# Retrieval stage: gate products as 64x32 tiles in four groups of 16 token pairs, scores in two halves

## The chip, the cores and the metric

The kernel runs on one core of one Trainium2 chip. The number that counts is device time in microseconds, the median of three runs; the profile is one further execution of the same program. Everything is float32, and a float32 product of the program stands in the trace as two LDWEIGHTS and two MATMUL (two passes).

## The reference, cut to what matters

The program is a whole two-layer perceiver block on 64 sequences of 32 tokens with 256 features (2048 tokens). The change touches one of its six parts, the feed-forward by retrieved experts of layer 0:

```python
sim = einsum('pbnhd,hkpd->pbnhk', q, keys)          # 2 x 8 heads x 64 keys per token
sx, ix = top_k(sim[0], 8);  sy, iy = top_k(sim[1], 8)
scores, pk = top_k(all pairs sx + sy, 8)            # 8 picks for each of 8 heads
indices = 64 * ix + iy, picked by pk                # one of 4096 experts
h = gelu(einsum('bnd,bnhkd->bnhk', x, down_embed[indices]))
out = einsum('bnhk,bnhkd->bnd', softmax(scores) * h, up_embed[indices])
```

A token has 64 picks, each an expert number and a weight.

## The kernel before, in words

Function `retrieve` does not gather experts. For each tile of 128 tokens it computes gelu(x · down) for all 4096 experts (`gh`, 128 expert rows x 32 expert columns x 128 tokens), multiplies it by a gate (the summed softmax weights, zero where an expert is not picked), and multiplies by the whole `up` table. The gate of a token is a product of two one-hot matrices over its picks: `row_hot` (pick x 128 rows) and `col_hot` (pick x column, times the weight).

Before the change two neighbouring tokens share one product: the 128 partitions hold the 64 picks of an even and the 64 of an odd token, `col_hot` has 64 columns (32 expert columns x parity of the token), and one matmul (L1262) contracts all 128 partitions into 128 x 64 gate values. 64 pairs make eight groups of eight; a group fills one PSUM bank, and two banks (5 and 6) take turns.

The stage is a software pipeline over 16 tiles, driven by `skewed`: in one step tile x is normalised, turned and scored, tile c (one behind) gets its hidden products and its picks, tile t (two behind) its gates, tile o (three behind) its output product. Steps 0 to 5 and the last three are written out; steps 6 to 15 are a hardware loop of five passes whose body is two steps. There is no planner: the order on each engine is as written, with semaphores between engines.

The step of TensorE (PE) has eight slices. In slice i, in this order: 4 `up` products of tile o (L1287, N=256), 8 `down` products of tile c (L1298, N=128), in slice 0 the turning of x (L1277), in slice 2 both score halves (L1270, banks 1 and 2), and gate group i (L1262), which waits for `weighted` of group i-2, for its `row_hot` and its `col_hot`. At the end of the step the picks are turned (L1310, bank 7).

VectorE (DVE), in slice i: `weigh(i-1)` (L1450: `gh` times a gate bank), `hot(i)` (L1436 compare; in even slices L1439, the near `row_hot`; L1442 times the weight), then a piece of the top-k of tile c (`share`). `scored` (L1454) is in slice 4. ScalarE (ACT), in slice i: in even slices 8 Abs (L1328, `rows_apart`) for the next odd group, the gelu of slice i (L1340), then Relu (L1334, the far `row_hot`). An Exp in slice 5 needs a table load each way.

Of the kernel before, what the change touches and what calls it, by code (L numbers as in the profile page):

```python
# [15 lines left out]
P = 128  # L16
# [7 lines left out]
C = 512  # L24
# [1165 lines left out]
def retrieve(nc, g, banks, n, pairs, offset, tables):  # L1190
# [7 lines left out]
    GROUPS, GP = 8, 8  # L1198
    CH = NE // GROUPS
    down, up = tables["down"], tables["up"]  # L1200
    with ExitStack() as ctx:
        s = Scope(nc, ctx, "s3e")
        sb = s.sb
        count, parity = sb("count", [P, K]), sb("parity", [P, 1])
# [13 lines left out]
        upper, low = sb("upper", [P, M]), sb("low", [P, M])  # L1218
# [4 lines left out]
        apart = sb("apart", [P, GP, P])  # L1223
        col_hot = sb("col_hot", [P, 2, GP, M])
# [5 lines left out]
        Y_BANK, S_BANK, H_BANK, G_BANK, T_BANK = 0, 1, 3, 5, 7  # L1230
# [3 lines left out]
        def half(t, i):  # L1234
            return t.b * (GROUPS // 2) + i // 2 + 1
# [16 lines left out]
        @block.tensor  # L1252
        def _(pe):
            def step(item):
                x, c, t, o = item(LAG_X), item(LAG_C), item(LAG_E), item(LAG_Y)

                def gate(i):
                    after(pe, weighted, group(t, i - 2))
                    pe.wait_ge(far_rows if i % 2 else near_rows, half(t, i))
                    pe.wait_ge(cols_ready, group(t, i))  # L1260
                    for j in range(GP):
                        mm = pe.matmul(banks[:, G_BANK + i % 2, j * M:(j + 1) * M], lhsT=row_hot[:, i % 2, j, :], rhs=col_hot[:, i % 2, j, :], start=True, stop=True)  # L1262
                    mm.then_inc(gate_ready, 1)

                def score():
                    pe.wait_ge(xT_ready, x.b + 1)
                    after(pe, sim_ready, x.b)
                    for j in range(2):
                        for k in range(KT):
                            mm = pe.matmul(banks[:, S_BANK + j, :], lhsT=xT[:, x.u, k, :], rhs=pairs[:, k, j * C:(j + 1) * C], start=k == 0, stop=k == KT - 1)  # L1270
                    mm.then_inc(sims, 1)

                def x_transposed():
                    pe.wait_ge(xn_ready, x.b + 1)
                    after(pe, picksT_ready, x.b - 1)
                    for k in range(KT):
                        mm = pe.transpose(banks[:, T_BANK, tok(k)], xn[:, x.u, tok(k)], g.ident[:])  # L1277
                    mm.then_inc(x_tr, 1)
                for i in range(GROUPS):
                    if o:  # L1280
                        if i == 0 and first(o):
                            pe.wait_ge(tables["up_loaded"], 16)
                        if i == 0:
                            pe.wait_ge(weighted, group(o, GROUPS - 1))
                            after(pe, added, o.b)
                        for e in range(i * CH, (i + 1) * CH):
                            mm = pe.matmul(banks[:, Y_BANK, 0:D], lhsT=gh[:, o.u, e, :], rhs=up[:, e, :], start=e == 0, stop=e == NE - 1)  # L1287
                        if i == GROUPS - 1:
                            mm.then_inc(summed, 1)
                    if c:  # L1290
                        if i == 0 and first(c):
                            pe.wait_ge(tables["down_loaded"], 16)
                        if i == 0:
                            pe.wait_ge(xT_ready, c.b + 1)
                        after(pe, gelu_ready, group(c, i - 2))
                        for e in range(CH):
                            for k in range(KT):
                                mm = pe.matmul(banks[:, H_BANK + i % 2, tok(e)], lhsT=down[:, k, i * CH + e, :], rhs=xT[:, c.u, k, :], start=k == 0, stop=k == KT - 1)  # L1298
                        mm.then_inc(hidden, 1)
# [6 lines left out]
                    if c and i == GROUPS - 1:  # L1306
                        pe.wait_ge(picks_ready, c.b + 1)
                        pe.wait_ge(xT_ready, c.b + 2 if x else NT)
                        for j in range(3):
                            mm = pe.transpose(banks[:, T_BANK, tok(j)], picks[:, j, :, :].rearrange("p r m -> p (r m)"), g.ident[:])  # L1310
                        mm.then_inc(picks_tr, 1)
            skewed(pe, NT, 3, step)

        @block.scalar
        def _(act):
            act.wait_ge(const_loaded, 48)
            act.wait_ge(set_up, 1)

            def step(item):
                x, c, t = item(LAG_X), item(LAG_C), item(LAG_E)  # L1320

                def rows_apart(i):
                    if i == 1:
                        act.wait_ge(picksT_ready, t.b + 1)
                    after(act, far_rows, half(t, i) - 1)
                    for j in range(GP):
                        q = i * GP + j
                        ins = act.activation(apart[:, j, :], number[:], ACT.Abs, bias=picksT[:, t.u, 0, q:q + 1], scale=-1.0)  # L1328
                    ins.then_inc(apart_ready, 1)

                def rows_hot(i):
                    act.wait_ge(apart_ready, half(t, i))
                    after(act, gate_ready, group(t, i - 2))
                    act.activation(row_hot[:, 1, :, :], apart[:], ACT.Relu, bias=one[:], scale=-1.0).then_inc(far_rows, 1)  # L1334
# [23 lines left out]
        def _(dve):  # L1358
            link = Link(dve, dve_link)
            dve.wait_ge(const_loaded, 48)  # L1360

            def step(item):
                x, c, t, o = item(LAG_X), item(LAG_C), item(LAG_E), item(LAG_Y)

                def best_of(first):
                    if first == 0:
                        dve.wait_ge(sim_ready, c.b + 1)
# [51 lines left out]
                def keys():  # L1419
# [6 lines left out]
                    link(dve.scalar_tensor_tensor(low[:], upper[:], -float(NE), key[:, 1, :], ALU.mult, ALU.add))  # L1426
                    dve.tensor_scalar(picks[:, 1, :, :], bc(low[:].unsqueeze(1), P, 2, M), 2.0, parity[:], ALU.mult, ALU.add).then_inc(picks_ready, 1)
# [3 lines left out]
                def hot(i):  # L1431
                    qs = slice(i * GP, (i + 1) * GP)
# [3 lines left out]
                    dve.tensor_tensor(col_hot[:, i % 2, :, :], bc(number[:, 0:M].unsqueeze(1), P, GP, M), bc(picksT[:, t.u, 1, qs].unsqueeze(2), P, GP, M),  # L1436
                                      ALU.is_equal).then_inc(cols_hit, 1)
                    if i % 2 == 0:
                        dve.tensor_tensor(row_hot[:, 0, :, :], bc(number[:].unsqueeze(1), P, GP, P), bc(picksT[:, t.u, 0, qs].unsqueeze(2), P, GP, P),  # L1439
                                          ALU.is_equal).then_inc(near_rows, 1)  # L1440
                    dve.wait_ge(cols_hit, group(t, i))
                    dve.tensor_tensor(col_hot[:, i % 2, :, :], col_hot[:, i % 2, :, :], bc(picksT[:, t.u, 2, qs].unsqueeze(2), P, GP, M),  # L1442
                                      ALU.mult).then_inc(cols_ready, 1)

                def weigh(i):
                    mine = gh[:, t.u, :, i * 2 * GP:(i + 1) * 2 * GP].rearrange("p e (q r) -> p e q r", r=2)
                    if i == 0:
                        dve.wait_ge(gelu_ready, group(t, GROUPS - 1))
                    dve.wait_ge(gate_ready, group(t, i))
                    dve.tensor_tensor(mine, banks[:, G_BANK + i % 2, :].rearrange("p (q e r) -> p e q r", q=GP, r=2), mine, ALU.mult).then_inc(weighted, 1)  # L1450
                def scored():
                    dve.wait_ge(sims, x.b + 1)
                    after(dve, sim_read, x.b - 1)
                    dve.tensor_tensor(sim[:, x.u, :, :].rearrange("p c k -> p (c k)"), banks[:, S_BANK:S_BANK + 2, :].rearrange("p n c -> p (n c)"), offset[:], ALU.add).then_inc(sim_ready, 1)  # L1454
# [5 lines left out]
                for i in range(GROUPS):  # L1460
# [9 lines left out]
                if o:  # L1470
                    dve.wait_ge(summed, o.b + 1)
# [6 lines left out]
            skewed(dve, NT, 3, step, link, 17)  # L1478
# [1297 lines left out]
```

## Time and profile before

| | us |
|---|---|
| three runs | 3247.96, 3250.59, 3251.38 |
| median | 3250.59 |
| the profiled execution, its own time | 3256.49 |
| its span, first to last instruction | 3254.7 |
| mean granted TensorE clock | 0.935 |
| busy: PE 2775.6, weight load (PEld) 2163.4, DVE 2127.2, ACT 1503.7, GpSimd 649.0 | |

The span is 1.8 us shorter than the profiled execution's time, and that execution is 5.9 us above the median. The retrieval lies from about 933 to 1737 us of the span. In the profile PE rows are matmuls, whose ends are modelled, and PEld rows are weight loads. In a merged row of several loads, the first starts at the row's start and the last ends at start plus duration.

### The profile page before, as it was taken

The numbers are of one execution on the slowest core, as the hardware profiler recorded it, in microseconds if no ns is written. First come the engines' busy times: TensorE is split into PE (matmuls) and PEld (weight loads), VectorE is DVE, ScalarE is ACT, GpSimd is POOL, SyncE is SP. The second block draws the span as 40 slices with busy tenths as digits, with TensorE's granted clock in tenths as the row PEclk, the third lists the DMA queues.
The fourth block names the chain that finished last, engine by engine and source line by source line (L and its number), as shares of the span: only waits on it lengthen the run. The fifth ranks groups of instructions, "written<-read, shape, count | busy, mean of one in ns | idle before, by whom it ended". The sixth has DMA issues, their size and how long they took to land. (4 is left out here: it accounts for less than half of the span.)

```text
span 3254.7 us, 64318 instructions
## 1 busy us (share of the span) xinstructions
PE 2775.6 (85%) x21884; PEld 2163.4 (66%) x21885; DVE 2127.2 (65%) x5161; ACT 1503.7 (46%) x4075; POOL 649.0 (20%) x809
## 2 busy tenths in 40 slices
PE   6699996999779999999997999995737777769993
PEld 3588884666668888889884777773323333569993
DVE  6588885666347777777772777775459999832222
ACT  3555552555224444444450777771366766113331
POOL 3355552122000000000000222220032222012224
PEclk8899998999879999999998999997859999969997
DMA  3122221000300000000000111111200000261112
GB/s 91 50 68 63 66 65 41 1 0 0 162 1 1 1 1 0 0 0 0 0 1 21 33 29 32 32 27 38 97 0 1 1 1 1 104 256 36 35 37 89
DMA packets 69088, 120.54 MB, mean 37 GB/s; under 512 B 10192, under 2 KB 51504, under 8 KB 64368
## 3 DMA queue, kind: packets, MB, share of 16 engines
q1 hardware_dynamic: 65568, 109.76, 10.2%
q0 software_dynamic: 3408, 9.31, 1.0%
q8 instruction: 67, 1.10, 0.1%
q14 instruction: 45, 0.37, 0.0%
HBM read 99.19 MB, written 17.69 MB: 36 GB/s over the span
## 5 line engine op out<-in xcount | busy, mean ns | idle before, releaser
L1262 PEld LDWEIGHTS s_ps<-s3e_col_hot,s3e_row_hot 128*128 128x128 f32 x2048 | 240.9, 192 | 36.6 <-issue 27.8
L1262 PE MATMUL s_ps<-s3e_col_hot,s3e_row_hot 128*128 128x64 f32 x2048 | 247.2, 274 | 21.1 <-DVE s3e_col_hot L1442 20.3
L1287 PE MATMUL s_ps<-s_up,s3e_gh 128*128 128x256 f32 x1024 | 252.8, 392 | 7.3 <-DVE s3e_gh L1450 7.3
L1298 PEld LDWEIGHTS s_ps<-s3e_xT,s_down 128*128 128x128 f32 x2048 | 249.9, 193 | 7.1 <-issue 1.1
L1298 PE MATMUL s_ps<-s3e_xT,s_down 128*128 128x128 f32 x2048 | 251.1, 277 | 0.0
L1340 ACT ACTIVATE s3e_gh<-s_ps 128x512 f32<-128x512 f32 x128 | 76.3, 597 | 364.1 <-PE s_ps L1298 363.9
L1287 PEld LDWEIGHTS s_ps<-s_up,s3e_gh 128*128 128x128 f32 x1024 | 188.1, 193 | 32.4 <-DVE s3e_gh L1450 10.5
L1450 DVE TENSOR_TENSOR s3e_gh<-s_ps,s3e_gh 128x512 f32<-128x512 f32 x128 | 88.3, 690 | 180.2 <-PE s_ps L1262 180.2
L1691 ACT ACTIVATE s4b_pr<-s4b_sc,s4b_nm 128x257 f32<-128x257 f32 x256 | 127.8, 503 | 114.9 <-DVE s4b_nm L1739 114.8
L2594 ACT ACTIVATE s6e_hT<-s_ps,s_b 128x128 f32<-128x128 f32 x312 | 84.9, 383 | 186.9 <-PE s_ps L2567 186.9
L2235 DVE SCALAR_TENSOR_TENSOR s5c_fresh<-s_ps,s5c_state 128x1024 f32<-128x1024 f32 x124 | 151.4, 1221 | 13.9 <-PE s_ps L2189 7.5
L191 POOL MEMSET s4q_half<- 128x1 f32 x1 | 0.1, 99 | 804.1 <-POOLq L2689 804.1
L1328 ACT ACTIVATE s3e_apart<-s3e_number,s3e_picksT 128x128 f32<-128x128 f32 x512 | 156.0, 388 | 1.6
L2567 PEld LDWEIGHTS s_ps<-s6e_xT,s6e_w 128*128 128x128 f32 x1248 | 146.7, 193 | 5.5 <-ACT s6e_xT L2598 3.5
L2567 PE MATMUL s_ps<-s6e_xT,s6e_w 128*128 128x128 f32 x1248 | 147.2, 277 | 2.9 <-ACT s6e_xT L2598 2.9
L2618 DVE TENSOR_TENSOR s6e_y<-s_ps,s_b 128x256 f32<-128x256 f32 x39 | 16.6, 425 | 198.5 <-PE s_ps L2581 198.5
L670 PE MATMUL p_ps<-s_wc,s1b_cT 96*128 96x256 f32 x512 | 128.1, 394 | 20.0 <-DMA s1b_cT<-ctxT 20.0
L2581 PE MATMUL s_ps<-s_w,s6e_hT 128*128 x624 | 141.2, 379 | 0.8 <-DVE s6e_y L2618 0.8
L2241 DVE TENSOR_TENSOR s5c_fresh<-s5c_fresh,s_ps 128x2048 f32<-128x2048 f32 x62 | 141.2, 2278 | 0.0
L2040 ACT ACTIVATE s5c_decay<-s5b_dt,s_rate 128x128 f32<-128x128 f32 x384 | 113.8, 389 | 45.9 <-PE s_ps L2189 44.2
L1643 PE MATMUL s_ps<-s4a_wv,s4b_cT 96*128 96x256 f32 x512 | 123.1, 384 | 4.4 <-DMA s4b_cT<-ctxT 4.4
L2581 PEld LDWEIGHTS s_ps<-s_w,s6e_hT 128*128 128x128 f32 x624 | 115.5, 190 | 15.3 <-issue 1.2
(428 smaller groups left out, 6630.9 us busy)
## 6 DMA issues: line engine op xcount, KB each, us to landing
s_w<-p_w SPq DMA_DIRECT2D x16, 1024.0 KB, 13.5
s4b_cT<-ctxT SPq DMA_DIRECT2D x64, 192.8 KB, 2.4
s1b_cx<-ctx SPq DMA_DIRECT2D x64, 192.0 KB, 2.7
s1b_cT<-ctxT SPq DMA_DIRECT2D x64, 192.0 KB, 2.9
s_results<-s6e_y SPq DMA_DIRECT2D x39, 128.0 KB
s_down<-p_down SPq DMA_DIRECT2D x1, 4096.0 KB, 22.0
s_up<-p_up SPq DMA_DIRECT2D x1, 4096.0 KB, 31.2
s_silu_z<-s5p_sz SPq DMA_DIRECT2D x4, 1024.0 KB, 4.5
```

Of the source, the lines that this page charges most:

```text
L670: mm = pe.matmul(banks[:, K_BANK + c.u, j * D:(j + 1) * D], lhsT=cT[:, c.u, k, tok(j)], rhs=wc[:, k, 0:D], start=k == 0, stop=k == 1)
L1262: mm = pe.matmul(banks[:, G_BANK + i % 2, j * M:(j + 1) * M], lhsT=row_hot[:, i % 2, j, :], rhs=col_hot[:, i % 2, j, :], start=True, stop= ...
L1287: mm = pe.matmul(banks[:, Y_BANK, 0:D], lhsT=gh[:, o.u, e, :], rhs=up[:, e, :], start=e == 0, stop=e == NE - 1)
L1298: mm = pe.matmul(banks[:, H_BANK + i % 2, tok(e)], lhsT=down[:, k, i * CH + e, :], rhs=xT[:, c.u, k, :], start=k == 0, stop=k == KT - 1)
L1328: ins = act.activation(apart[:, j, :], number[:], ACT.Abs, bias=picksT[:, t.u, 0, q:q + 1], scale=-1.0)
L1643: mm = pe.matmul(banks[:, V_BANK, j * D:(j + 1) * D], lhsT=cT[:, d.u, k, tok(j)], rhs=wv[:, k, :], start=k == 0, stop=k == 1)
L1691: ins = act.activation(pr[:, e.u, n, :], sc[:, e.u, n, :], ACT.Exp, bias=nm[:, e.u, n:n + 1], accum_out=sums[:, bass.ds(e.b, 1), n])
L2040: return act.activation(decay[:, t % 2:t % 2 + steps, k, :, n, :], steps_of(dt, k, t, steps), ACT.Exp, scale=rate[:, k, n:n + 1])
L2235: dve.scalar_tensor_tensor(part_of(fresh, h, part, 2), banks[:, D_BANK:D_BANK + 2, :].rearrange("p j d -> p (j d)"), floor, part_of(state, ...
L2241: dve.tensor_tensor(part_of(fresh, h, 0, HG), part_of(fresh, h, 0, HG), banks[:, I_BANK:I_BANK + HG, :].rearrange("p j d -> p (j d)"), ALU ...
L2567: mm = pe.matmul(banks[:, H_BANK + 2 * m.u + f // 4, tok(f % 4)], lhsT=w[:, m.u, k, tok(f)], rhs=xT[:, m.u, k, :], start=k == 0, stop=k == ...
L2581: mm = pe.matmul(banks[:, Y_BANK, 0:D], lhsT=hT[:, o.u, f, :], rhs=w2[:, bass.ds(e, 1), f, :], start=f == 0, stop=f == FT - 1)
```

## The change

- Gates: each token has a product of its own. Four column tiles of 32 expert rows times two row tiles of 64 partitions make 8 products of 64x32 weights with N=32 per pair, in place of one of 128x128 with N=64. The even token writes one bank, the odd token another. `col_hot` has 32 columns; the parity input and `low` are gone.
- Groups: four of 16 pairs instead of eight of 8, one every second slice, each in two banks (4/5 and 6/7). In every group the first 8 pairs have a near `row_hot` (DVE) and the last 8 a far one (ACT), so that the far one is needed by every group.
- PE's order: `down` before `up` in each slice; the gate's waits (`gate_inputs`) stand ahead of `up` in odd slices, the gate itself at the slice's end.
- ACT's gelu of slice i now waits for `up` of slice i too, since both tiles share the `gh` buffer.
- Scores: halves in slices 2 and 5 through bank 1, which also serves both turnings; `scored` in slices 3 and 7. The picks' turning waits for the second half to be read.

```diff
-    GROUPS, GP = 8, 8
-    CH = NE // GROUPS
+    SLICES, GROUPS, GP, HP = 8, 4, 16, 8
+    CH = NE // SLICES
+    GC = 32
...
-        col_hot = sb("col_hot", [P, 2, GP, M])
+        col_hot = sb("col_hot", [P, 2, GP, NE])
...
-        Y_BANK, S_BANK, H_BANK, G_BANK, T_BANK = 0, 1, 3, 5, 7
+        Y_BANK, T_BANK, H_BANK, G_BANK = 0, 1, 2, 4
...
-            for dst, src in ((count, "count8"), (parity, "parity"), (number, "row_no")):
+            for dst, src in ((count, "count8"), (number, "row_no")):
...
+                def gate_inputs(i):
+                    after(pe, weighted, group(t, i - 2))
+                    pe.wait_ge(near_rows, group(t, i))
+                    pe.wait_ge(far_rows, group(t, i))
+                    pe.wait_ge(cols_ready, group(t, i))
+
                 def gate(i):
-                    after(pe, weighted, group(t, i - 2))
-                    pe.wait_ge(far_rows if i % 2 else near_rows, half(t, i))
-                    pe.wait_ge(cols_ready, group(t, i))
                     for j in range(GP):
-                        mm = pe.matmul(banks[:, G_BANK + i % 2, j * M:(j + 1) * M], lhsT=row_hot[:, i % 2, j, :], rhs=col_hot[:, i % 2, j, :], start=True, stop=True)
+                        for g in range(P // GC):
+                            for r in range(2):
+                                ms, cs = slice(r * M, (r + 1) * M), slice(g * GC, (g + 1) * GC)
+                                mm = pe.matmul(banks[cs, G_BANK + 2 * (i % 2) + r, j * NE:(j + 1) * NE], lhsT=row_hot[ms, i % 2, j, cs], rhs=col_hot[ms, i % 2, j, :],
+                                               start=True, stop=True)
                     mm.then_inc(gate_ready, 1)
...
+                    if t and i % 2:
+                        gate_inputs(i // 2)
...
                     if x and i == 2:
-                        score()
-                    if t:
-                        gate(i)
+                        score(0)
+                    if x and i == 5:
+                        score(1)
+                    if t and i % 2:
+                        gate(i // 2)
                     if c and i == GROUPS - 1:
...
-                        pe.wait_ge(xT_ready, c.b + 2 if x else NT)
+                        pe.wait_ge(sim_ready, 2 * c.b + 4 if x else 2 * NT)
...
-                for i in range(GROUPS):
+                for i in range(SLICES):
                     if t and i % 2 == 0:
-                        rows_apart(i + 1)
+                        rows_apart(i // 2)
                     if c:
-                        act.wait_ge(hidden, group(c, i))
+                        act.wait_ge(hidden, part_of(c, i))
+                        if o:
+                            act.wait_ge(summed, part_of(o, i))
...
                     if t and i % 2 == 0:
-                        rows_hot(i + 1)
+                        rows_hot(i // 2)
...
-                for i in range(GROUPS):
-                    if t:
+                for i in range(SLICES):
+                    if t and i % 2 == 0:
                         if i:
-                            weigh(i - 1)
-                        hot(i)
-                    if x and i == 4:
-                        scored()
+                            weigh(i // 2 - 1)
+                        hot(i // 2)
+                    if x and i == 3:
+                        scored(0)
+                    if x and i == 7:
+                        scored(1)
```

## Rows read from the trace of the kernel before

**Rows 1.** The page, costliest groups: the loads of the gate and of `down`.

```profile
L1262 PEld LDWEIGHTS s_ps<-s3e_col_hot,s3e_row_hot 128*128 128x128 f32 x2048 | 240.9, 192 | 36.6 <-issue 27.8
L1298 PEld LDWEIGHTS s_ps<-s3e_xT,s_down 128*128 128x128 f32 x2048 | 249.9, 193 | 7.1 <-issue 1.1
```

**Rows 2.** Windows: one step of the loop, from one turning of picks to the next.

```profile
core 0: us, PE busy (x) PEld busy (x) DVE busy (x) ACT busy (x) POOL busy (x), PEclk, DMA share, GB/s
1299.79:1347.84 48.05, 47.10 (x336) 42.90 (x334) 36.53 (x124) 22.11 (x50) 0.00 (x0) 1.00 0.00 0
```

**Rows 3.** Timeline, weight loads of one slice: start, duration, name, idle before.

```profile
1325.69 1.60 PEld L1287 LDWEIGHTS s_ps<-s_up,s3e_gh 128*128 128x128 f32 x8
1327.32 1.97 PEld L1298 LDWEIGHTS s_ps<-s3e_xT,s_down 128*128 128x128 f32 x16
1329.20 1.87 PEld L1262 LDWEIGHTS s_ps<-s3e_col_hot,s3e_row_hot 128*128 128x128 f32 x16
1330.99 1.60 PEld L1287 LDWEIGHTS s_ps<-s_up,s3e_gh 128*128 128x128 f32 x8
```

**Rows 4.** Timeline where two steps meet.

```profile
1299.77 0.69 DVE L1450 TENSOR_TENSOR s3e_gh<-s_ps,s3e_gh 128x512 f32<-128x512 f32 x1 [1.76 <-PE s_ps L1262]
1300.51 1.59 PEld L1287 LDWEIGHTS s_ps<-s_up,s3e_gh 128*128 128x128 f32 x8 [0.69 <-DVE s3e_gh L1450]
```

**Rows 5.** Timeline, loads of a burst of 128x32 weights, N=32, in phase 1.

```profile
302.49 0.22 PEld L662 LDWEIGHTS p_ps<-s1b_pT,s1b_vv 128*32 128x32 f32 x16 [0.39 <-ACT s1b_pT L723]
...
302.84 0.17 PEld L662 LDWEIGHTS p_ps<-s1b_pT,s1b_v 128*32 128x32 f32 x7
303.05 0.30 PEld L670 LDWEIGHTS p_ps<-s_wc,s1b_cT 96*128 96x128 f32 x2
```

**Rows 6.** Groups by form: busy us, mean ns of one load in the two bursts.

```profile
L662 PEld LDWEIGHTS p_ps<-s1b_pT,s1b_vv 128*32 128x32 f32 x2048 | 29.1, 112 | 25.6 <-ACT s1b_pT L723 13.6 <-issue 12.0
L1676 PEld LDWEIGHTS s_ps<-s4b_kT,s4b_qb 32*64 32x64 f32 x1024 | 15.4, 129 | 44.8 <-DVE s4b_nm L1739 26.8 <-issue 13.7 <-ACT s4b_kT L1703 4.3
```

**Rows 7.** Timeline, loads of a burst with row tiles (32x64 weights) in phase 4.

```profile
2002.22 0.24 PEld L1676 LDWEIGHTS s_ps<-s4b_kT,s4b_qb 32*64 32x64 f32 x16 [0.95 <-DVE s4b_nm L1739]
```

**Rows 8.** Groups by form, 1300 to 1670 us: DVE's and ACT's parts around the gate.

```profile
L1450 DVE TENSOR_TENSOR s3e_gh<-s_ps,s3e_gh 128x512 f32<-128x512 f32 x62 | 42.8, 690 | 84.9 <-PE s_ps L1262 84.9
L1442 DVE TENSOR_TENSOR s3e_col_hot<-s3e_col_hot,s3e_picksT 128x512 f32<-128x512 f32 x62 | 42.7, 689 | 1.1
L1436 DVE TENSOR_TENSOR s3e_col_hot<-s3e_number,s3e_picksT 128x512 f32<-128x512 f32 x62 | 42.2, 681 | 0.0
L1439 DVE TENSOR_TENSOR s3e_row_hot<-s3e_number,s3e_picksT 128x1024 f32<-128x1024 f32 x31 | 37.8, 1219 | 0.0
```

**Rows 9.** Timeline, ACT and DVE beside the slice of Rows 3.

```profile
1324.71 2.43 ACT L1328 ACTIVATE s3e_apart<-s3e_number,s3e_picksT 128x128 f32<-128x128 f32 x8
...
1328.29 0.68 DVE L1442 TENSOR_TENSOR s3e_col_hot<-s3e_col_hot,s3e_picksT 128x512 f32<-128x512 f32 x1
...
1329.51 0.60 ACT L1340 ACTIVATE s3e_gh<-s_ps 128x512 f32<-128x512 f32 x1 [2.37 <-PE s_ps L1298]
1330.01 1.14 ACT L1334 ACTIVATE s3e_row_hot<-s3e_apart,s3e_one 128x1024 f32<-128x1024 f32 x1
```

**Rows 10.** DMA queue of instructions, first 1040 to 1250 us, then 1252 to 1650 us.

```profile
q8 instruction: 12, 0.20, 0.4%
...
q8 instruction: 1, 0.02, 0.0%
```

**Rows 11.** DMA issues, the shortest time to landing: size, then us.

```profile
s6r_rw<-p_rw SPq DMA_DIRECT2D x1, 8.0 KB, 1.6
```

**Rows 12.** Timeline at the start of the retrieval.

```profile
933.44 0.42 SPq L1246 DMA_DIRECT2D s3e_parity<-parity  x1
...
935.78 0.41 DVE L169 TENSOR_SCALAR s3e_xn<-x_rows,s_mv,s_rstd 128x256 f32<-128x256 f32 x1 [20.61 <-DMA s3e_number<-row_no]
```

More of the change, by code:

```diff
@@ L1203, in retrieve @@
         sb = s.sb
-        count, parity = sb("count", [P, K]), sb("parity", [P, 1])
+        count = sb("count", [P, K])
         number = sb("number", [P, P])
@@ L1217, in retrieve @@
         ex, den, rden = sb("ex", [P, H, K]), sb("den", [P, H]), sb("rden", [P, H])
-        upper, low = sb("upper", [P, M]), sb("low", [P, M])
+        upper = sb("upper", [P, M])
         picks = sb("picks", [P, 3, 2, M])
@@ L1222, in retrieve @@
         row_hot = sb("row_hot", [P, 2, GP, P])
-        apart = sb("apart", [P, GP, P])
-        col_hot = sb("col_hot", [P, 2, GP, M])
+        apart = sb("apart", [P, HP, P])
+        col_hot = sb("col_hot", [P, 2, GP, NE])
         gh = sb("gh", [P, U, NE, P])
@@ L1229, in retrieve, with part_of @@
             "apart_ready near_rows far_rows cols_hit cols_ready gate_ready weighted hidden gelu_ready summed added")
[L1230 removed]
+        Y_BANK, T_BANK, H_BANK, G_BANK = 0, 1, 2, 4
         LAG_X, LAG_C, LAG_E, LAG_Y = range(4)
         block = ctx.enter_context(nc.Block())
[L1234 to L1235 removed]
+        def part_of(t, i):
+            return t.b * SLICES + i + 1
         def group(t, i):
@@ L1255, in step, with score @@
                 x, c, t, o = item(LAG_X), item(LAG_C), item(LAG_E), item(LAG_Y)
+                def gate_inputs(i):
[3 more added lines that the diff above has]
+                    pe.wait_ge(cols_ready, group(t, i))
                 def gate(i):
-                    after(pe, weighted, group(t, i - 2))
-                    pe.wait_ge(far_rows if i % 2 else near_rows, half(t, i))
-                    pe.wait_ge(cols_ready, group(t, i))
                     for j in range(GP):
-                        mm = pe.matmul(banks[:, G_BANK + i % 2, j * M:(j + 1) * M], lhsT=row_hot[:, i % 2, j, :], rhs=col_hot[:, i % 2, j, :], start=True, stop=True)
-                    mm.then_inc(gate_ready, 1)
[L1265 to L1270, printed above, removed]
+                        for g in range(P // GC):
[3 more added lines that the diff above has]
+                                               start=True, stop=True)
+                    mm.then_inc(gate_ready, 1)
+                def score(j):
+                    if j:
+                        pe.wait_ge(sim_ready, 2 * x.b + 1)
+                    else:
+                        pe.wait_ge(xT_ready, x.b + 1)
+                    for k in range(KT):
+                        mm = pe.matmul(banks[:, T_BANK, :], lhsT=xT[:, x.u, k, :], rhs=pairs[:, k, j * C:(j + 1) * C], start=k == 0, stop=k == KT - 1)
                     mm.then_inc(sims, 1)
@@ L1275, in x_transposed @@
                     after(pe, picksT_ready, x.b - 1)
+                    after(pe, sim_ready, 2 * x.b)
                     for k in range(KT):
@@ L1278, in x_transposed @@
                     mm.then_inc(x_tr, 1)
-                for i in range(GROUPS):
+                for i in range(SLICES):
+                    if c:
+                        if i == 0 and first(c):
+                            pe.wait_ge(tables["down_loaded"], 16)
+                        if i == 0:
+                            pe.wait_ge(xT_ready, c.b + 1)
+                        after(pe, gelu_ready, part_of(c, i - 2))
+                        for e in range(CH):
+                            for k in range(KT):
+                                mm = pe.matmul(banks[:, H_BANK + i % 2, tok(e)], lhsT=down[:, k, i * CH + e, :], rhs=xT[:, c.u, k, :], start=k == 0, stop=k == KT - 1)
+                        mm.then_inc(hidden, 1)
+                    if t and i % 2:
+                        gate_inputs(i // 2)
                     if o:
@@ L1287, in step @@
                             mm = pe.matmul(banks[:, Y_BANK, 0:D], lhsT=gh[:, o.u, e, :], rhs=up[:, e, :], start=e == 0, stop=e == NE - 1)
[L1288 to L1299, printed above, removed]
+                        mm.then_inc(summed, 1)
                     if x and i == 0:
@@ L1315, in _ @@
         def _(act):
-            act.wait_ge(const_loaded, 48)
+            act.wait_ge(const_loaded, 32)
             act.wait_ge(set_up, 1)
             def step(item):
-                x, c, t = item(LAG_X), item(LAG_C), item(LAG_E)
+                x, c, t, o = item(LAG_X), item(LAG_C), item(LAG_E), item(LAG_Y)
                 def rows_apart(i):
-                    if i == 1:
+                    if i == 0:
                         act.wait_ge(picksT_ready, t.b + 1)
-                    after(act, far_rows, half(t, i) - 1)
-                    for j in range(GP):
-                        q = i * GP + j
+                    after(act, far_rows, group(t, i) - 1)
+                    for j in range(HP):
+                        q = i * GP + HP + j
                         ins = act.activation(apart[:, j, :], number[:], ACT.Abs, bias=picksT[:, t.u, 0, q:q + 1], scale=-1.0)
@@ L1331, in rows_hot @@
                 def rows_hot(i):
-                    act.wait_ge(apart_ready, half(t, i))
+                    act.wait_ge(apart_ready, group(t, i))
                     after(act, gate_ready, group(t, i - 2))
-                    act.activation(row_hot[:, 1, :, :], apart[:], ACT.Relu, bias=one[:], scale=-1.0).then_inc(far_rows, 1)
-                for i in range(GROUPS):
+                    act.activation(row_hot[:, i % 2, HP:GP, :], apart[:], ACT.Relu, bias=one[:], scale=-1.0).then_inc(far_rows, 1)
+                for i in range(SLICES):
                     if t and i % 2 == 0:
-                        rows_apart(i + 1)
+                        rows_apart(i // 2)
                     if c:
-                        act.wait_ge(hidden, group(c, i))
+                        act.wait_ge(hidden, part_of(c, i))
+                        if o:
+                            act.wait_ge(summed, part_of(o, i))
                         act.activation(gh[:, c.u, i * CH:(i + 1) * CH, :].rearrange("p e q -> p (e q)"), banks[:, H_BANK + i % 2, :], ACT.Gelu_apprx_tanh).then_inc(gelu_ready, 1)
                     if t and i % 2 == 0:
-                        rows_hot(i + 1)
+                        rows_hot(i // 2)
                     if x and i == 0:
@@ L1425, in keys @@
                     dve.scalar_tensor_tensor(picks[:, 0, :, :], bc(key[:, 0, :].unsqueeze(1), P, 2, M), 2.0, bc(upper[:].unsqueeze(1), P, 2, M), ALU.mult, ALU.add)
-                    link(dve.scalar_tensor_tensor(low[:], upper[:], -float(NE), key[:, 1, :], ALU.mult, ALU.add))
-                    dve.tensor_scalar(picks[:, 1, :, :], bc(low[:].unsqueeze(1), P, 2, M), 2.0, parity[:], ALU.mult, ALU.add).then_inc(picks_ready, 1)
+                    dve.scalar_tensor_tensor(picks[:, 1, :, :], bc(upper[:].unsqueeze(1), P, 2, M), -float(NE), bc(key[:, 1, :].unsqueeze(1), P, 2, M),
+                                             ALU.mult, ALU.add).then_inc(picks_ready, 1)
                 pieces = (lambda: best_of(H), candidates, lambda: places_of(0), lambda: places_of(H), top_of, positions, hits, soften, keys)
@@ L1431, in hot @@
                 def hot(i):
-                    qs = slice(i * GP, (i + 1) * GP)
+                    qs, near = slice(i * GP, (i + 1) * GP), slice(i * GP, i * GP + HP)
                     if i == 0:
@@ L1447, in weigh, with scored @@
                     if i == 0:
-                        dve.wait_ge(gelu_ready, group(t, GROUPS - 1))
+                        dve.wait_ge(gelu_ready, part_of(t, SLICES - 1))
                     dve.wait_ge(gate_ready, group(t, i))
[L1450 to L1454, printed above, removed]
+                    both = banks[:, G_BANK + 2 * (i % 2):G_BANK + 2 * (i % 2) + 2, :]
+                    dve.tensor_tensor(mine, both.rearrange("p r (q e) -> p e q r", q=GP), mine, ALU.mult).then_inc(weighted, 1)
+                def scored(j):
+                    dve.wait_ge(sims, 2 * x.b + j + 1)
+                    if j == 0:
+                        after(dve, sim_read, x.b - 1)
+                    dve.tensor_tensor(sim[:, x.u, j * H:(j + 1) * H, :].rearrange("p c k -> p (c k)"), banks[:, T_BANK, :], offset[:, j * C:(j + 1) * C], ALU.add).then_inc(sim_ready, 1)
                 if x:
@@ L1459, in step @@
                     best_of(0)
-                for i in range(GROUPS):
-                    if t:
+                for i in range(SLICES):
+                    if t and i % 2 == 0:
                         if i:
-                            weigh(i - 1)
-                        hot(i)
-                    if x and i == 4:
-                        scored()
+                            weigh(i // 2 - 1)
[4 more added lines that the diff above has]
+                        scored(1)
                     if c:
@@ L1477, in step @@
                     dve.bn_stats(g.stats[:, o.b, :], X[:, o.b, :])
-            skewed(dve, NT, 3, step, link, 17)
+            skewed(dve, NT, 3, step, link, 16)
 def phase4(nc, g):
```

17 lines of the change are left out of this document (8 added, 9 removed).

## The prediction

> **What bounds the kernel now.** I read the page's groups first, then one step by windows, then the timeline of one slice. In the groups the gate's weight loads take as long as those of `down`, 241 and 250 us, though its products have N=64 against 128 [rows 1]: a 128x128 load costs 118 ns (240.9 / 2048), and N=64 hides under it. The windows say whose time it is: a step lasts 48.05 us, PE is busy for 47.10 at full clock, DVE for 36.5, ACT for 22.1 [rows 2]. So whatever leaves PE shortens the step until DVE, at 36.5, or a chain through DVE and ACT is late. In the slice, loads start at 1325.69 (`up`), 1327.32 (`down`), 1329.20 (gate) and 1330.99 (`up`): 1.63 + 1.88 + 1.79 = 5.30 us [rows 3]. Two gate groups are 3.58 us; four such pairs make 14.3 us of a step. The only real gap is where steps meet: `up` waits 0.69 us for the last `weigh` [rows 4].
>
> **The new gate on PE.** A group of 16 pairs is 16 x 8 products = 128, two passes each = 256 loads and 256 matmuls, in place of 32 and 32. The trace has no 64x32 burst. The nearest is 128x32 with N=32 [rows 5]: 48 passes, first load at 302.49, the last seven begin at 302.84 and end 0.17 later; a load of this form lasts 0.112 [rows 6], so the last starts at 302.90: 0.41 us for 47 steps, 8.7 ns each. Its first 16 need (0.22 - 0.11)/15 = 7.3 ns, and so do 16 loads over row tiles (0.24 - 0.13, /15) [rows 6, 7], so row tiles bring no penalty. From first load to the next line's load are 0.56 us for 48, 11.7 ns each with the change of shape at the end. Bounds for a group: 256 x 7.3 = 1.9 us and 256 x 11.7 = 3.0 us. I take 256 x 8.7 = 2.2, plus 0.15 at the exit (0.56 - 0.41) and 0.1 at the entry, whose load can't slip under the matmul before: 2.5 us. Against 3.58 a group saves 1.08 us, a step 4.3 us.
>
> The burst in the trace is short, and its 8.7 ns a pass need tiles that work side by side [rows 5]. The Trainium skill, TensorEngine Tiling (Array Packing), section Instruction Overhead, says that each matmul has about 60 cycles of overhead and that one shouldn't take a tiling factor from a dimension that is already small. This change does just that; by that rule, an estimate, a pass would be 25 ns and a group 6.4 us. The row shows passes of a third of that, so it speaks against; it stays as a rival.
>
> **Instruction supply.** This is the term that I can't read directly. PE's instructions per step are 336 + 334 = 670 now [rows 2]; the change takes 4 x 64 away and adds 4 x 512: 2462. Between 1040 and 1250 us, written-out steps and the loop's first pass, the instruction queue moved 12 packets of 16 KB, one per 17.5 us, or 17.5 x 670/48 = 244 instructions: a packet is about 256 instructions of 64 bytes. From 1252 to 1650 us, the other four passes of the loop, it moved one [rows 10]. So the body of 1340 instructions is kept. A body of 4924 may not be; then each pass fetches again, 10 packets a step. A group's 512 instructions are two packets used up in 2.2 us, 1.1 us each. A packet takes 0.4% x 16 x 210 / 12 = 1.12 us of a DMA engine [rows 10], just even. If the next is asked for only when the one before it is entered, the time to landing counts: the shortest in the trace is 1.6 us, for 8 KB [rows 11]. If 0.3 of that is data (a guess) and 1.12 stands in its place, it is 2.4. Then one packet per group comes late by 2.4 - 1.1 = 1.3 us. Bounds: 0 and 1.3 us per group. I take 0.45, nearer to the packet's own row, since some instructions are queued ahead. A step: +1.8 us. Each jump back of the loop, four of them, may wait for its target: bounds 0 and 2.4, I take 1.5: +6 us in all.
>
> The Trainium skill, Runtime: NRT & Kernel Launch, section Instruction fetch mechanics, gives PE room for 2048 instructions, refilled in blocks of 256, the next fetched while the current runs, and a wait at a taken branch outside that window. The trace agrees on the block (244) and doesn't show the room. By it the loop is refetched and the wait is not zero.
>
> **The waits put ahead of `up`.** In a double slice, PE's loads now run `down` 0 to 1.88, `up` to 3.51, `down` to 5.39, then the gate's waits with `up` and the gate queued behind them. The far `row_hot` is ready when? ACT's gelu of the even slice waits for `up`'s matmuls, whose end is 0.06 + 1.95 after its first load at 1.88: 3.9. Gelu to Relu takes 0.50 and the Relu 1.14 [rows 9]: 5.55, the wait seen at 5.6 and the first load at 5.65 to 5.7. That is 0.3 late. In slice 0 the turning of x, in slice 2 the score half give cover, so 2 of 4 double slices pay: +0.6 us a step; bounds 0 and 4 x 0.3. The 8 Abs (2.43) start after the odd gelu of the double slice before, and are done long before 3.9.
>
> On DVE: gate end, `weigh` over 1024 columns 1.22 (as L1439, the same width), compare 0.6, near rows 1.15, product 0.69 [rows 8], ready about 4.0 after the double slice starts, needed at 5.4. In slice 0 the statistics, the normalisation and eight MAX8 come first, but also the turned picks and x on PE; ready about 0.6 us ahead of need. Bounds: 0, and 0.5 us a step if it isn't; I take 0.
>
> **Where steps meet.** `down` (1.88 us) now stands before `up`, and `weigh` grows from 0.69 to 1.22: it ends about 1.35 us after the gate, the picks' turning and `down` cover 2.3. The gap of 0.69 goes [rows 4]: -0.6 us a step. The picks' turning waits for `scored(1)` in slice 7, behind `keys` on DVE; DVE has 1 us to spare there, bounds 0 and 1 us.
>
> **The rest.** DVE loses 4 x (0.68 + 0.69) for `col_hot`, 8 x 0.69 becomes 4 x 1.22 for `weigh`, `low` goes (0.2), two half `scored` cost 0.2 more: 36.5 to about 30.4 us, below the new step. It is worth nothing by itself; it only keeps DVE from bounding. The score passes are the same eight; their bank is read between the halves, two slices apart. Parity's DMA goes from the start, 0.42 us of issue ahead of the load that DVE waits for [rows 12]: -0.4 us once.
>
> **Sum.** A step with a tile in t: -4.3 + 1.8 + 0.6 - 0.6 = -2.5 us, 16 such steps: -40. Loop jumps +6, parity -0.4: -34 us. Against the profiled execution's own 3256.5 that gives 3222.5; it stands 5.9 above the median of 3250.6, which I forecast: 3217.
>
> **Rivals.**
> 1. Supply is no limit. Loads as above, no late packet, no wait at jumps: -4.3 us a step, 16 x = -69: 3182; at 7.3 ns a pass 3160. For it: PE ran 96 instructions in 0.41 us without a hitch [rows 5]. Against: those fit a queue, 512 don't. Chance 0.17.
> 2. The other side: instruction supply bounds the gate. One late packet per group. From 0.95 us on (64 x 0.95 = 61 of delay, plus 6 to 10 for jumps, against 69 saved) the change is not faster; at 1.3 it gives 64 x 1.3 + 4 x 2.4 - 69 = +24: 3274. For it: the landing time [rows 11] and a body 3.7 times as long. Against: a packet's 1.12 us. Chance 0.27.
> 3. The inputs bound: far rows, `col_hot` or the picks come about 1 us late in each double slice, because a wait ahead of `up` stops everything behind it. 64 x 0.7 of delay beyond the sum: 3262. For it: already now `col_hot` ends at 1328.97 and its gate starts at 1329.20 [rows 3, 9]. Against: the sums above. Chance 0.1.
> 4. The tiles' loads run one after another: 32 columns cost a quarter of the 118 ns of 128 [rows 1], 29 ns a pass, 7.5 us a group: 64 x (7.5 - 2.5) = +320 from the sum: 3537. Against: 8.7 ns in the burst [rows 5]. Chance 0.04. (The page on tiling would have it so, near enough.)
>
> My forecast has 0.42: late packets of 0.2 to 0.8 us per group, 3195 to 3243. A measurement can tell about 0.2%, 6.5 us, from no change. Faster (below 3244): 0.42 + 0.17, less 0.05 for the upper edge = 0.54. Within: 0.05 from there and 0.05 from rivals 2 and 3: 0.1. Slower: 0.36. The range is 3172 to 3285: it leaves out rival 4 and the tails of 1 and 2.
>
> **What would show it.** A loop step of 45.5 us by the turning of picks (43.7 in rival 1, about 49.5 in rival 2). L1262's successor with 16384 loads, 256 of a group within 2.2 us; a hole of over 0.5 us amid a group, near an instruction packet, speaks for supply, and instruction packets every 4 to 5 us all through the loop say that the body isn't kept. No hole and 8.7 ns: rival 1. The wait of `up` on ACT's far rows in slices 5 and 7, about 0.3 us each. No wait of `up` on `weigh` where steps meet. DVE near 30 us a step. The forecast is wrong if passes run at over 12 ns in an unbroken burst, or if holes exceed 0.9 us.

## The result: 3383.8 us, 4.1% slower

The changed kernel takes 3383.81 us (median of four runs, 3378.16 to 3386.72) against 3249.47 for the kernel before on the same chip: ratio 1.0411, 95% interval 1.0393 to 1.0429. The forecast was 3217, faster, with a range up to 3285. It was wrong in its sign and in its range. The profiled execution took 3378.16 us with a span of 3376.4, which is 121.7 above the span before.

First the page of the changed kernel: weight loads of the gate (L1269), `down` (L1298) and `up` (L1309). Behind the bars stand busy us and mean ns, then idle time ahead and what ended it.

```profile
L1269 PEld LDWEIGHTS s_ps<-s3e_col_hot,s3e_row_hot 64*32 64x32 f32 x16384 | 151.9, 106 | 162.5 <-issue 162.2
L1298 PEld LDWEIGHTS s_ps<-s3e_xT,s_down 128*128 128x128 f32 x2048 | 286.5, 221 | 36.1 <-issue 32.4
L1309 PEld LDWEIGHTS s_ps<-s_up,s3e_gh 128*128 128x128 f32 x1024 | 198.5, 204 | 40.8 <-issue 11.1
```

The `up` loads of the kernel before, which the groups ahead don't show:

```profile
L1287 PEld LDWEIGHTS s_ps<-s_up,s3e_gh 128*128 128x128 f32 x1024 | 188.1, 193 | 32.4 <-DVE s3e_gh L1450 10.5 <-issue 0.6
```

With [rows 1] these rows say where the time went. Gate: busy -89.0, idle +125.9. `down`: busy +36.6, idle +29.0. `up`: +10.4 and +8.4. The sum is +121.3 us. That it equals the growth of the span, 121.7, is in part chance: the retrieval, from its first weight load to the end of its last, grew from 798.8 to 929.9 us, by 131.1, and the rest of the program, which the change doesn't touch, was 9.4 shorter in this execution. The other 10 us of the retrieval lie in its smaller products and where rows overlap. So the gate's loads became cheaper, as forecast, and the gate's idle time, nearly all "issue" (waiting for nothing that the profile shows), grew by 126 us.

Two steps of it by windows, the columns as in [rows 2]. The first (step 7) ends the loop's first pass, the second (step 8) begins with the first jump back.

```profile
1233.44:1286.98 53.54, 46.08 (x1231) 40.29 (x1229) 30.86 (x111) 22.12 (x50) 0.00 (x0) 0.94 0.01 3
1286.98:1346.79 59.81, 46.75 (x1238) 40.35 (x1230) 30.85 (x111) 22.12 (x50) 0.00 (x0) 0.91 0.01 3
```

PE is now busy for 46 of 53 to 60 us, where it was busy for 47.10 of 48.05; DVE fell from 36.5 to 30.9, as forecast (30.4). The timeline of the loads shows the holes. Columns: start, duration, instructions, idle before.

```profile
1280.71 1.59 PEld L1309 LDWEIGHTS s_ps<-s_up,s3e_gh 128*128 128x128 f32 x8
1282.64 1.50 PEld L1269 LDWEIGHTS s_ps<-s3e_col_hot,s3e_row_hot 64*32 64x32 f32 x166 [0.33 <-issue]
1286.08 0.86 PEld L1269 LDWEIGHTS s_ps<-s3e_col_hot,s3e_row_hot 64*32 64x32 f32 x90 [1.95 <-issue]
1286.98 0.31 PEld L1323 LDWEIGHTS s_ps<-x_ident,s3e_picks 128*128 128x128 f32 x3
1291.68 3.48 PEld L1298 LDWEIGHTS s_ps<-s3e_xT,s_down 128*128 128x128 f32 x16 [4.39 <-issue]
1295.04 3.00 PEld L1309 LDWEIGHTS s_ps<-s_up,s3e_gh 128*128 128x128 f32 x8
1298.07 0.36 PEld L1287 LDWEIGHTS s_ps<-x_ident,s3e_xn 128*128 128x128 f32 x2
1298.39 1.86 PEld L1298 LDWEIGHTS s_ps<-s3e_xT,s_down 128*128 128x128 f32 x16
```

The burst of 256 loads runs at 8 to 9 ns each, stops for 1.95 us, and goes on. Over all 64 bursts the mean length, from the start of the first load to that of the last, is 4.36 us; the shortest, unbroken, take 2.14, and 60 of the 64 have at least one hole. So the holes cost 64 x 2.22 = 142 us in all. The second thing is at 1286.98: the loop jumps back, and the next `down` starts 4.4 us later and takes 3.48 us instead of 1.86. Windows of the stretches with the clock (third column from the end): the wait at the jump, `down` and `up` behind it, the next slice.

```profile
1286.98:1291.60 4.62, 0.55 (x11) 0.31 (x3) 4.50 (x14) 3.09 (x10) 0.00 (x0) 0.57 0.04 7
1291.60:1298.10 6.50, 6.42 (x24) 5.86 (x25) 4.01 (x28) 0.00 (x0) 0.00 (x0) 0.52 0.01 3
1298.39:1301.80 3.41, 3.41 (x26) 3.23 (x25) 0.00 (x0) 1.91 (x3) 0.00 (x0) 1.00 0.00 0
```

A granted clock of 0.52 is the lower of the two levels, 1.2 GHz, for nearly the whole stretch: it fell while PE idled at the jump, stayed low while `down` and `up` ran, and is 1.00 in the slice behind them. In the kernel before a step of the loop had it at 1.00 [rows 2]. Over the whole retrieval the trace has the lower level for 177 us, where the kernel before had it for 24. Last, the instruction queue from 1300 to 1700 us, all in the loop:

```profile
q8 instruction: 72, 1.18, 1.3%
```

72 packets, one per 5.6 us, where the kernel before had one in the last four passes of its loop, 400 us [rows 10]: the loop's body is no longer kept.

### The profile page after: what moved, and what is told of

Same layout as the page of the kernel before. It is cut to its first block and busy times, and to the rows that moved or that the text cites. A ratio compares the mean times of both kernels' runs of the same rounds, so it can differ in the third digit from the quotient of the medians.

```text
span 3376.4 us, 92832 instructions
## 1 busy us (share of the span) xinstructions
PE 2774.1 (82%) x36220; PEld 2133.2 (63%) x36221; DVE 2035.5 (60%) x4969; ACT 1503.9 (45%) x4075; POOL 645.4 (19%) x809
## 5 line engine op out<-in xcount | busy, mean ns | idle before, releaser
L1298 PE MATMUL s_ps<-s3e_xT,s_down 128*128 128x128 f32 x2048 | 300.2, 308 | 21.2 <-issue 21.2
L1298 PEld LDWEIGHTS s_ps<-s3e_xT,s_down 128*128 128x128 f32 x2048 | 286.5, 221 | 36.1 <-issue 32.4
L1465 DVE TENSOR_TENSOR s3e_gh<-s_ps,s3e_gh 128x1024 f32<-128x1024 f32 x64 | 78.4, 1225 | 377.7 <-PE s_ps L1269 377.7
L1269 PE MATMUL s_ps<-s3e_col_hot,s3e_row_hot 64*32 64x32 f32 x16384 | 166.9, 203 | 128.3 <-issue 128.0
L1309 PE MATMUL s_ps<-s_up,s3e_gh 128*128 128x256 f32 x1024 | 261.5, 402 | 8.2 <-ACT s3e_row_hot L1347 4.1
L1269 PEld LDWEIGHTS s_ps<-s3e_col_hot,s3e_row_hot 64*32 64x32 f32 x16384 | 151.9, 106 | 162.5 <-issue 162.2
L1309 PEld LDWEIGHTS s_ps<-s_up,s3e_gh 128*128 128x128 f32 x1024 | 198.5, 204 | 40.8 <-issue 11.1
```

Of the source, the lines that this page charges most:

```text
L1269: mm = pe.matmul(banks[cs, G_BANK + 2 * (i % 2) + r, j * NE:(j + 1) * NE], lhsT=row_hot[ms, i % 2, j, cs], rhs=col_hot[ms, i % 2, j, :], s ...
```

## The experiments

The theory, S in what follows, is supply: PE's instructions come in packets of 256, and a burst that uses up more than one waits for the next; a body that isn't kept waits at each jump as well. Rivals: the form of the tiles itself is slow, the new order of work is to blame, or the waits for the inputs are. A ratio is against the kernel before on the same chip: it took 3254.77 us beside the first four runs and 3256.29 beside the last three.

**Tiles of 64x64, half the instructions.** All else stays: same data, waits and order.

```diff
-    GC = 32
+    GC = 64
```

> The changed kernel with GC = 64: gate tiles of 64x64 instead of 64x32, so 128 passes (256 instructions) a group instead of 256 (512). Theory S (instruction supply): a block of 256 instructions is asked for when the one before is entered and lands about 3.4 us later, so a burst that holds only one block boundary mostly has no hole; a group takes about 2.1 us, a step about 42 to 43 us, jumps back of the loop still cost about 8 us each (1438 instructions a step, 2876 a body); about 3190 us. Rival E (the engine stalls by itself in bursts of small tiles): a hole of over 2 us in every burst stays, over 3330 us.

Measured: 3161.73 us, ratio 0.9717 (0.9701 to 0.9733). Page row, one double slice, and a jump back, from its timeline:

```profile
L1269 PEld LDWEIGHTS s_ps<-s3e_col_hot,s3e_row_hot 64*64 64x64 f32 x8192 | 126.2, 135 | 28.2 <-issue 27.8
```

```profile
1144.07 1.96 PEld L1269 LDWEIGHTS s_ps<-s3e_col_hot,s3e_row_hot 64*64 64x64 f32 x128 [0.33 <-issue]
1146.06 1.86 PEld L1298 LDWEIGHTS s_ps<-s3e_xT,s_down 128*128 128x128 f32 x16
...
1296.38 0.31 PEld L1323 LDWEIGHTS s_ps<-x_ident,s3e_picks 128*128 128x128 f32 x3
1300.49 3.08 PEld L1298 LDWEIGHTS s_ps<-s3e_xT,s_down 128*128 128x128 f32 x16 [3.80 <-issue]
1303.45 2.06 PEld L1309 LDWEIGHTS s_ps<-s_up,s3e_gh 128*128 128x128 f32 x8
```

One edit takes some 220 us away, 28 more than expected. The burst is 256 instructions, as long as one packet, so it crosses at most one end of a packet; 61 of the 64 bursts have no hole and three have one of 0.2 to 0.3 us. A pass of 64x64 is slower (14.3 ns against 8.4), yet the burst is even shorter, since there are half as many. Three of the four jumps cost 5.4 to 5.6 us (steps of 46.7 to 46.9 against 41.3): 3.7 to 3.8 of waiting, the rest at the lower clock. At the fourth the wait was 3.3 us, `down` and `up` behind it ran at full speed, and the step was 3.3 us longer. Expected were 8 us each.

**PE's steps written out, tiles 64x32.** No jump is left on PE; the bursts are the same.

```diff
-            skewed(pe, NT, 3, step)
+            for v in range(NT + 3):
+                step(lambda s: Item(0, v - s) if 0 <= v - s < NT else None)
```

> The changed kernel with TensorE's 19 retrieval steps written out, no loop on that engine. Theory S: the four jumps back (4.4 us of wait, then 3.5 us of products at the half clock) go, the holes inside bursts stay: 3350 to 3360 us. Rival J (a loop has nothing to do with it, the longer loop steps come from something else): no change, 3384 us. If written-out code starves more than a loop, slower.

Measured: 3366.47 us, ratio 1.0352 (1.0330 to 1.0375). Steps 6 to 15, those of the loop before, now take 53.6 to 58.6 us; 17 us went, less than expected, and the holes stayed (140 us over the 64 bursts, 142 with the loop). Its timeline holds the clearest row of the study:

```profile
1338.20 0.90 PEld L1269 LDWEIGHTS s_ps<-s3e_col_hot,s3e_row_hot 64*32 64x32 f32 x95 [0.33 <-issue]
1339.66 1.17 PEld L1269 LDWEIGHTS s_ps<-s3e_col_hot,s3e_row_hot 64*32 64x32 f32 x128 [0.57 <-issue]
1343.14 0.32 PEld L1269 LDWEIGHTS s_ps<-s3e_col_hot,s3e_row_hot 64*32 64x32 f32 x33 [2.30 <-issue]
```

Between two holes lie exactly 128 loads, with their matmuls 256 instructions: one packet. It is used up in 1.17 us, and the next is there 3.48 us after it began. So a packet comes late by 2.3 us, and neither the pairs' data nor a semaphore has a boundary there.

The whole trace says the same. Number all of PE's instructions in order of time: the 67 holes of over 0.15 us inside the bursts stand at numbers that leave a remainder of 113 or 114 by 256, every one of them. With the packets of the instruction queue beside them, the delay can be taken apart. For the 54 holes of over 1 us (medians), the packet's transfer starts 1.0 us after PE entered the packet before, takes 1.1 us, and PE goes on 1.4 us after its end: 3.5 us from one packet's first instruction to the next one's, 3.2 to 4.0 in nine of ten.

**Tiles 64x32, the burst in two halves.** The first 8 pairs follow `down` of the odd slice, the last 8 its `up`. The waits for the near rows and the columns move up with them, to the last product of `down`; the far rows are waited for ahead of `up` as before.

```diff
-                def gate(i):
-                    for j in range(GP):
+                def gate(i, h):
+                    for j in range(h * HP, (h + 1) * HP):
...
+                            if e == CH - 1 and t and i % 2:
+                                gate_inputs(i // 2)
...
-                        gate_inputs(i // 2)
+                        if not c:
+                            gate_inputs(i // 2)
+                        gate(i // 2, 0)
+                        pe.wait_ge(far_rows, group(t, i // 2))
...
-                        gate(i // 2)
+                        gate(i // 2, 1)
```

> The changed kernel with each 64x32 burst of 16 pairs in two halves of 8 pairs, one after down and one after up of the odd slice; number and form of the instructions are the same (the far rows are waited for ahead of up). Theory S: 1.6 us of slow code between the halves covers part of a block's landing: the hole shrinks from 2.3 to about 0.7 to 1 us, four more changes of tile form a step cost 1 us: about 3300 us. Rival E: the holes depend on the number of small passes alone and stay: 3390 us or more.

Measured: 3239.84 us, ratio 0.9954 (0.9937 to 0.9971): 60 us better than expected, and with the same tiles and as many products 144 us better than the change. From its timeline:

```profile
1150.98 1.18 PEld L1268 LDWEIGHTS s_ps<-s3e_col_hot,s3e_row_hot 64*32 64x32 f32 x128
1152.20 1.59 PEld L1314 LDWEIGHTS s_ps<-s_up,s3e_gh 128*128 128x128 f32 x8
1154.12 0.38 PEld L1268 LDWEIGHTS s_ps<-s3e_col_hot,s3e_row_hot 64*32 64x32 f32 x35 [0.33 <-issue]
1154.82 0.88 PEld L1268 LDWEIGHTS s_ps<-s3e_col_hot,s3e_row_hot 64*32 64x32 f32 x93 [0.32 <-issue]
```

The 1.6 us of `up`, which need only 16 instructions, give the next packet time. Over the retrieval 52 holes are left, half of them under 0.5 us and 12 over 1 us; together they are 40 us, where the change had 142. The number of instructions alone is not the matter, their density is, and the form of the tiles is out as a rival, since it is the same here.

**The old products in the new frame.** 128x128 products and the parity column as before, in four groups, with the new order, waits and score halves.

```diff
-                        for g in range(P // GC):
-                            for r in range(2):
-                                ms, cs = slice(r * M, (r + 1) * M), slice(g * GC, (g + 1) * GC)
-                                mm = pe.matmul(banks[cs, G_BANK + 2 * (i % 2) + r, j * NE:(j + 1) * NE], lhsT=row_hot[ms, i % 2, j, cs], rhs=col_hot[ms, i % 2, j, :],
-                                               start=True, stop=True)
+                        mm = pe.matmul(banks[:, G_BANK + 2 * (i % 2) + j // HP, (j % HP) * M:(j % HP + 1) * M], lhsT=row_hot[:, i % 2, j, :], rhs=col_hot[:, i % 2, j, :],
+                                       start=True, stop=True)
```

> The changed kernel with its four groups of 16 pairs, its order, its waits ahead of up, its far rows in every group and its score halves, but with the old products (128x128 weights, N=64, parity column) in the gate. Theory S: the frame is about neutral, the step 47 to 48.5 us, 3235 to 3255 us, so all the loss is in the tiles. Rival F (the frame's new waits cost): above 3290 us.

Measured: 3242.85 us, ratio 0.9966 (0.9956 to 0.9976), steps of 47.64 us against 48.05. The frame is worth 0.4 us a step in our favour, so neither the new order nor the waits carry the loss. Its group of 16 pairs takes

```profile
1251.15 3.76 PEld L1266 LDWEIGHTS s_ps<-s3e_col_hot,s3e_row_hot 128*128 128x128 f32 x32
```

3.76 us from the start of the first load to the end of the last. The same measure for two groups of eight in the kernel before is 2 x 1.87 = 3.74 [rows 3]; the 3.58 of the prediction runs from first load to the next line's load.

**64x64 tiles, written out.** The first two edits together.

> Tiles of 64x64 and TensorE's retrieval steps written out. Theory S: the four long steps (46.7 us against 41.3) become 41.3 to 41.8, about -20 us against the 64x64 kernel's 3161.7: 3140 to 3145 us. Rival J (the long steps are not from the loop's jump): 3160 us.

Measured: 3144.17 us, ratio 0.9660 (0.9644 to 0.9676), as expected: most steps take 41.74 us, and the long steps at the jumps are gone. The steps between, 41.27 us in the loop, became 0.5 us longer; why, no run shows.

**Row tiles only: weights of 64x128.** Two products per pair; the burst is half a packet.

```diff
-    GC = 32
+    GC = 128
```

> The changed kernel with GC = 128: one token's product as 64x128 weights, two row tiles, 64 passes (128 instructions) a group; a step has about 926 loads and products, a loop body 1852. Theory S: a body under 2048 instructions is kept, so no long loop steps and no instruction packets after the first pass; the group's time is then the loads': 64 x 118 = 7.5 us if the row tiles' loads don't overlap (step 62 us, 3470 us), 3.8 us if two overlap (step 47.5 us, 3240 us). Rival: the body isn't kept, packets go on all through the loop and every second step is 5 us longer.

Measured: 3346.59 us, ratio 1.0266 (1.0237 to 1.0294). The expectation of 3240 failed, in two points. The body of about 1860 instructions (a step has 1442 with 64x64 tiles, here 4 x 128 fewer) isn't kept either: steps of 54.5 and 58.1 us alternate and there were 32 packets from 1300 to 1700 us. So a body of 1340 loads and matmuls was kept and one of about 1860 wasn't (all of PE's instructions counted: 1390 and 1892); no run lies between. The group itself came as expected for two overlapping tiles, 3.7 to 3.8 us. But the clock fell. Windows of a double slice: gate, two slices, gate, the `down` and `up` behind it.

```profile
1290.70:1294.39 3.69, 3.69 (x65) 3.65 (x64) 0.00 (x0) 2.93 (x9) 0.00 (x0) 1.00 0.02 4
1294.39:1303.34 8.95, 8.95 (x55) 7.29 (x53) 7.08 (x31) 1.63 (x2) 0.00 (x0) 1.00 0.00 0
1303.34:1307.55 4.21, 4.21 (x65) 4.15 (x65) 0.00 (x0) 2.92 (x9) 0.00 (x0) 0.86 0.01 4
1307.55:1313.68 6.13, 6.13 (x25) 5.64 (x24) 5.92 (x25) 0.00 (x0) 0.00 (x0) 0.54 0.00 0
```

Two row tiles do overlap: 64 loads take 3.65 us, 57 ns a load against 118 of a full one, and in the trace they start in pairs, 7 ns and 105 ns apart. That leaves a group hardly cheaper than the old one. Within a burst and behind it the clock then goes to the lower level, though PE is marked busy without a gap; the retrieval has it for 235 us, against 24 in the kernel before, and the loads of `down` are busy for 307.7 us instead of 249.9. In the written-out run with 64x64 tiles it is 8 us. I can't say why from these rows.

**64x64, written out, far rows first.** One wait was left: `up` stood still for the far `row_hot`, because ACT makes it behind the gelu, which waits for `up` of the slice before. ACT now makes it first.

```diff
                         rows_apart(i // 2)
+                        rows_hot(i // 2)
...
-                    if t and i % 2 == 0:
-                        rows_hot(i // 2)
```

> The 64x64 kernel written out, and on ScalarE the Relu of the far rows ahead of the even slice's gelu instead of behind it. The prediction's step on the waits ahead of up (far rows 0.3 us late in two to three of four double slices) says that this takes 0.7 to 1.2 us off a step: 3125 to 3132 us. Rival: the far rows' lateness is hidden anyway, same as without the swap, 3140 to 3145 us.

Measured: 3125.57 us, ratio 0.9601 (0.9585 to 0.9617), the best of all. One step by windows:

```profile
1242.97:1283.80 40.83, 40.83 (x724) 35.93 (x718) 30.86 (x111) 22.57 (x50) 0.00 (x0) 1.00 0.01 2
```

PE is busy for all 40.83 us; DVE, at 30.9, is far from the bound.

## Why the prediction was wrong

**The step that failed** is the term "I take 0.45, nearer to the packet's own row, since some instructions are queued ahead", 1.8 us a step. It measured 2.2 us per group, 8.9 a step, and lies beyond the upper bound of 1.3 as well. The prediction had named holes of over 0.9 us as a sign that it is wrong. Rival 2 had the right mechanism (one late packet per group, slower from 0.95 us on); I gave it 0.27 and priced it at 3274. The bound was too low because I took the time to landing from an 8 KB transfer that SP issues, 1.6 us [rows 11], and put 2.4 for a packet. The written-out run shows 3.5 from one packet's first instruction to the next one's: 1.1 is the transfer, as put, but 1.0 passes before it starts and 1.4 between its end and PE's next instruction, and the prediction had 1.3 for both. With 3.5 - 1.1 = 2.4 in the same formula the forecast would have been slower by some 90 us before the clock. The row on the transfer time of a packet [rows 10] says what it costs a DMA engine, not when it is asked for and when PE can run it; choosing the value nearest to it was the error. The hole per burst with 64x32 tiles, its absence with 64x64 tiles, the 128 loads between holes, the shrinking when `up` stands between the halves, and the packets' times beside the holes show the cause together. No row shows the request for a packet itself, only that its transfer starts 1.0 us after the packet before is entered.

The Trainium skill, Runtime: NRT & Kernel Launch, section Instruction fetch mechanics, says that the next block is fetched while the current one runs and that crossing a boundary is "mostly hidden". The block of 256 agrees with the 128 loads and their matmuls between two holes; "mostly hidden" holds for the 64x64 bursts and fails for 512 instructions in 2.14 us. For the wait at a taken branch the section sets a window of two pages, 512 instructions; the prediction put PE's room of 2048 in its place. The traces agree with neither figure: a body of 1390 instructions brought one packet in its last four passes [rows 10], and one of 1892 brought 32 packets in 400 us.

**The jumps** were taken at 1.5 us each, bounds 0 and 2.4. They cost 4.4, 4.3, 4.3 and 3.9 us of waiting, and behind it `down` and `up` run 2.6 to 3.0 us longer at the lower clock (3.48 and 3.00 us against 1.86 and 1.59 at the first). That the body isn't kept was forecast; the check named for it, packets all through the loop, came out.

**The clock** was not in my sum at all. The loads of `down` and `up` are busy for 47.0 us more than before (36.6 + 10.4), in stretches behind holes and jumps. With 64x64 tiles, written out, far rows first, they are at 243 and 186 us, where before had 250 and 188.

**The account of the error.** The forecast for the profiled execution was 3222.5 us, it took 3378.2: 155.7 more. By the page's rows, measured against forecast:

| | measured, us | forecast, us | difference, us |
|---|---|---|---|
| idle in and ahead of the gate (late packets) | +125.9 | +28.8 | +97 |
| busy loads of the gate | -89.0 | -68.8 | -20 |
| idle ahead of `down` (jumps, in the main) | +29.0 | +6 | +23 |
| busy loads of `down` and `up` (lower clock) | +47.0 | 0 | +47 |
| idle ahead of `up` (far rows, meeting of steps) | +8.4 | 0 (+9.6 - 9.6) | +8 |

Together 155 us. Another 10 us are in the retrieval's smaller products and overlaps, which I don't break down, and the rest of the program was 9.4 shorter. Of the 29.0 us ahead of `down` the four jumps are 16.8. The far rows' wait stands in two places: 4.1 us by name ahead of the matmuls of `up`, and part of the 11.1 of "issue" ahead of its loads, since with 64x64 tiles that "issue" fell from 20.9 to 8.9 us when ACT made the far rows first.

**What was right.** Passes of 8.4 ns in an unbroken burst (2.14 us over 255 steps), 8.7 taken; row tiles and column tiles side by side, so that rival 4 is out; the step-meeting gap (waits of `up` on `weigh` fell from 10.5 to 2.3 us); DVE at 30.9. Rival 1 is out by the holes. The estimate of 25 ns a pass, from the 60 cycles per matmul of the Trainium skill, TensorEngine Tiling (Array Packing), section Instruction Overhead, isn't borne out by this trace, with its 8.4. Two small readings were off without effect: the compare and the near rows take 0.68 and 1.22 us [rows 8], not 0.6 and 1.15. Rival 3 was half there: its wait is small, but worth 0.91 us a step once the holes are gone, as the last experiment shows.

## What to carry to other kernels

Before splitting a matmul into tiles, count instructions per microsecond: a float32 64x32 product is four of them, and a burst that runs through a whole packet of 256 went on only about 3.5 us after that packet began. Choose the tile by the time of the burst with its supply, not by the pass: here 64x64 at 14.3 ns beats 64x32 at 8.4 ns by 220 us of 3384. A hardware loop stops being free once its body isn't kept; then try the engine's steps written out (17 us less in both pairs of runs here), and split dense bursts with long instructions between the parts.

## What the runs showed that I had not expected

- The supply: 256 instructions per 3.48 us in a burst that runs dry; a single packet's worth, 128 loads of 64x64 in 1.96 us, had no hole of over 0.3 us.
- A jump back to a body that isn't kept: 3.3 to 4.4 us of wait. A body of about 1340 loads and matmuls on PE was kept, one of about 1860 was not.
- Load times in a burst: 8.4 ns (64x32, eight tiles), 14.3 ns (64x64, four), 57 ns (64x128, two), 118 ns (128x128) [rows 1].
- A PE that is marked busy throughout can still get the lower clock: 0.54 behind a burst of 64x128 weights. It did not behind 64x64 bursts. Why is open.
